# Rotary attention inputs with features in the order (dimension, head): half the rotary products, and six pack loads a unit for twelve

## The chip, the cores and the metric

The kernel runs on one core of a Trainium2 chip. The metric is the device time of one execution in microseconds (us). Names of engines: PE is the matrix engine (TensorE), DVE the VectorE, ACT the ScalarE, POOL the GpSimd, SP the SyncE, which here only issues DMAs. A "q" behind an engine's name (SPq, ACTq) is its DMA-issuing side. TensorE's clock has two levels, 1.2 and 2.4 GHz, and the profile gives the granted share of the higher one.

## The reference, cut to what matters

```python
# x: (8, 512, 256)   ctx: (8, 1601, 256)   16 heads of 16 dimensions
h = x + cross_attention(layernorm(x), ctx)        # weights Wq, Wk, Wv, Wo with biases
z = rmsnorm(layernorm(h), g1)
q, k, v = z @ wq, z @ wk, z @ wv                   # 16 heads of 16
q = q * cos + rotate_half(q) * sin                 # rotate_half([a, b]) = [-b, a], halves of 8
k = k * cos + rotate_half(k) * sin
a = causal_softmax(q @ k.T * 16 ** -0.5) @ v @ wo
... # residuals, a second rmsnorm, top-2 of 8 experts (256 -> 704 -> 256), residuals
```

## The kernel before

The work is done in stages with a barrier between them: prepare_weights, project_inputs, attention (cross), invert_denominators, project_self, attention (self, causal), invert_denominators, finish_self, route, experts. Matrices of fp32 precision are multiplied in bf16 where scores are made: every query and key feature is cut into three bf16 parts (high, middle, low), and the scores take six of the nine pairs of parts in one product over 6 x 16 = 96 rows of the contraction, with three more rows that subtract the row's maximum (99 in all).

project_inputs writes the parts to DRAM as k_parts and q_parts, shape (batch, 3 parts, 256 features, tokens). A feature's number is head * 16 + dimension.

attention works through 32 units, each one batch and four heads. For a unit, `load_kq` (L568 on) fills k_pack and q_pack, of 128 partitions x 4 heads x tokens. Each of the six pairs of parts takes 16 partitions (the dimension of the head), and each is filled by one DMA for the key and one for the query: 12 DMAs of 16 partitions, with a run of 3202 B (key, cross attention) or 1024 B (query, and key in self attention) for each head. SP issues, in order for each unit: the value loads for a later unit (L581, L585; runs of 64 B), the 12 pack loads for the unit three ahead (L570, L573), the store of the unit before (L590). Four pack buffers exist.

On PE the "pieces" (L637) are scores in the order (query, key) of which DVE takes the maxima (L718). They are spread by `step_of` over the steps of the unit before. POOL splits the maxima in three bf16 parts, PE turns them (L646), ACT copies them (L799) and sends them by a DMA of its own queue to rows 96 to 98 of q_pack (L804, the max-row transfer, 12 KB). The first scores of the next unit (L656) wait for that transfer; ACT then takes exponentials (L793), and PE the products with the values (L671). In self attention POOL also starts one load of expert weights a unit (L1855), on a third queue.

project_self handles a batch in each turn of a software pipeline (`turns`): each engine has a fixed list of parts, each for a batch some turns back. DVE's list is: subtract_high of k (b-3), residual (b-1), divide (b), rope of q (b-2), layer_norm (b-1), rms_inverse (b-1), subtract_high of q (b-2), rope of k (b-2). PE's list is: turn_rows (b-1), out_product (b), q_products (b-1), v_product (b-1), k_products (b-1). The rotation of halves is put into the weights: prepare_weights makes wq_rot and wk_rot, and rope_products multiplies with wq and wq_rot into ps_a and ps_b, which queries and keys share. DVE multiplies ps_a by the cosines and ps_b by the sines, POOL adds (L1137), ACT and DVE make the parts, SP stores them.

Of the kernel before, what the change touches and what calls it, by code (L numbers as in the profile page):

```python
# [17 lines left out]
GH = 4  # L18
# [19 lines left out]
K_PARTS = (0, 1, 2, 0, 1, 0)  # L38
Q_PARTS = (0, 0, 0, 1, 1, 2)
PAIRS = len(K_PARTS)  # L40
# [29 lines left out]
def prepare_weights(nc, w, keep):  # L70

    with ExitStack() as stack:
        p = Prog(nc, stack, "prep_")
        raw = {n: p.sb(f"raw_{n}", [P, KC, DIM]) for n in ("Wq", "Wk", "Wv", "Wo")}
# [6 lines left out]
        rot_ready = p.sem("rot_ready")  # L81

        with nc.Block() as block:
# [6 lines left out]
            @block.scalar  # L90
            def _(act):

                for n in ("bq", "bk", "g1"):
                    act.dma_start(keep[n][:, :], w[n].rearrange("(c p) -> p c", p=P),
                                  allow_slow_non_contiguous=True).then_inc(small_in, 16)
                for n in ("bv", "bo", "g2"):
                    act.dma_start(keep[n][:, :], w[n].partition_broadcast(P)).then_inc(small_in, 16)
                for n in ("wq", "wk", "wv", "wo"):
                    act.dma_start(keep[n][:, :, :], w[n].rearrange("(c p) o -> p c o", p=P)).then_inc(small_in, 16)
                act.dma_start(keep["w_router"][:, :, :], w["w_router"].rearrange("(c p) e -> p c e", p=P))\  # L100
                   .then_inc(small_in, 16)
                act.wait_ge(small_in, 16 * 11)

                nc.scalar.mul(keep["bq"][:, :], keep["bq"][:, :], SCALE)

                for src, dst in (("wq", "wq_rot"), ("wk", "wk_rot")):
                    s = keep[src][:, :, :].rearrange("p c (h t d) -> p (c h) t d", t=2, d=HD // 2)
                    d = keep[dst][:, :, :].rearrange("p c (h t d) -> p (c h) t d", t=2, d=HD // 2)
                    nc.scalar.mul(d[:, :, 0, :], s[:, :, 1, :], -1.0)
                    last = nc.scalar.copy(d[:, :, 1, :], s[:, :, 0, :])  # L110
                last.then_inc(rot_ready, 1)
                act.wait_ge(rot_ready, 1)
# [12 lines left out]
            @block.vector  # L125
            def _(dve):
                nc.vector.memset(keep["ln_eps"][:, :], LN_EPS)
                nc.vector.memset(keep["rms_eps"][:, :], RMS_EPS)
                for k, n in enumerate(("WqT", "WkT", "WvT", "WoT")):
                    dve.wait_ge(turned_ready, k + 1)  # L130
                    nc.vector.tensor_copy(keep[n][:, :, :], turned[k][:, :, :])
# [311 lines left out]
def attention(nc, q_parts, k_parts, v_rows, out_rows, kv, causal, keep, units, beside=None):  # L443
# [28 lines left out]
    with ExitStack() as stack:  # L472
# [30 lines left out]
        KQ = 16 * 2 * PAIRS  # L503
# [10 lines left out]
        class Unit:  # L514


            def __init__(self, i, r):
# [4 lines left out]
                self.rows = slice(g * GR, (g + 1) * GR)  # L522
# [42 lines left out]
        with nc.Block() as block:  # L565
            @block.sync
            def _(sp):
                def load_kq(v):  # L568
                    for r in range(PAIRS):
                        sp.dma_start(kp[v.buf][r * HD:(r + 1) * HD, :, :],  # L570
                                     k_parts[v.batch, K_PARTS[r], v.rows, :].rearrange("(j d) n -> d j n", d=HD))\
                          .then_inc(kq_in[v.buf], 16)
                        sp.dma_start(qp[v.buf][r * HD:(r + 1) * HD, :, :],  # L573
                                     q_parts[v.batch, Q_PARTS[r], v.rows, :].rearrange("(j d) n -> d j n", d=HD))\
# [305 lines left out]
def project_self(nc, x_in, out_rows, inverse, x1_rows, h0_rows, q_parts, k_parts, v_rows, keep, batches):  # L880


    with ExitStack() as stack:
# [19 lines left out]
        ps_a = p.ps("ps_a", [P, KC, SEQ])  # L903
        ps_b = p.ps("ps_b", [P, KC, SEQ])
# [30 lines left out]
        with nc.Block() as block:  # L935
# [43 lines left out]
            def _(pe):  # L979
# [17 lines left out]
                def rope_products(w, b):  # L997
                    pe.wait_ge(rope_read, b * 2 + w + 1)
                    for ps, weights in ((ps_a, ("wq", "wk")[w]), (ps_b, ("wq_rot", "wk_rot")[w])):
                        for o in range(KC):  # L1000
                            for i in range(KC):
                                last = nc.tensor.matmul(ps[:, o, :], keep[weights][:, i, o * P:(o + 1) * P],
                                                        xT[:, i, :], start=(i == 0), stop=(i == KC - 1))
# [21 lines left out]
            def _(dve):  # L1025
                for s in (on_ready, x1_ready, rope_read, *rest_ready):
                    dve.sem_inc(s, 1)

# [28 lines left out]
                def rope(w, b):  # L1057
                    dve.wait_ge(rope_done, b * 2 + w + 1)
                    dve.wait_ge(full_ready[w], b + 1)
                    for i in range(KC):  # L1060
                        nc.vector.tensor_tensor(t1[w][:, i, :], ps_a[:, i, :], keep["cos_" + "qk"[w]][:, :], ALU.mult)
                        last = nc.vector.tensor_tensor(t2[w][:, i, :], ps_b[:, i, :], keep["sin_" + "qk"[w]][:, :],
                                                       ALU.mult)
# [59 lines left out]
            def _(pool):  # L1123
# [10 lines left out]
                def add_and_split(w, b):  # L1134
                    pool.wait_ge(rope_read, b * 2 + w + 2)
# [682 lines left out]
def shape_constants():  # L1818
# [6 lines left out]
    cos = np.tile(np.cos(angle).T, (P // (HD // 2), 1)).astype(np.float32)  # L1825
    sin = np.tile(np.sin(angle).T, (P // (HD // 2), 1)).astype(np.float32)
# [35 lines left out]
KEEP_SHAPES = {"WqT": 0, "WkT": 0, "WvT": 0, "WoT": 0, "wq": 0, "wk": 0, "wv": 0, "wo": 0, "wq_rot": 0, "wk_rot": 0}  # L1862
# [80 lines left out]
```

## Time and profile before

| | |
|---|---|
| median of 3 runs | 3095.22 us (3091.45 to 3095.96) |
| the profiled execution, its own time | 3085.21 us |
| span of its profile | 3083.4 us |
| busy: PE, DVE, ACT, POOL | 87%, 59%, 47%, 19% |
| mean granted clock of TensorE | 0.928 |

The profile is of one execution. Its span is from the first to the last instruction. Where the page names what ended an idle time, that is the last of the things waited for. The stages lie, by the first loads of each, at 0 to 20 us (weights), to 290 (project_inputs), to 1581 (cross attention), to 1829 (the first inversion and project_self), to 2222 (self attention), to 2440 (finish_self and route) and to the end (experts).

### The profile page before, as it was taken

What the parts mean: (1) busy time and instruction counts of PE and PEld (TensorE: products, weight loads), DVE (VectorE), ACT (ScalarE), POOL (GpSimd) and SP (SyncE); (2) the same over time, 40 slices, a digit from 0 to 9 for tenths busy, and PEclk for the clock granted to TensorE, in tenths of its full rate; (3) what the DMA queues carried; (4) which work ended last, traced back from release to release, by engine and by line L of the source; (5) the groups of instructions that cost most, each with busy time, mean ns of one, the idle gap of its engine ahead of it and who ended that gap; (6) DMA issues with size and microseconds to landing.
All of it is one profiled execution on the core that took longest, in us unless ns stands there. A gap on an engine that the chain in (4) does not pass through costs nothing. (4 is left out here: it accounts for less than half of the span.)

```text
span 3083.4 us, 58524 instructions
## 1 busy us (share of the span) xinstructions
PE 2679.9 (87%) x14782; PEld 1368.5 (44%) x14783; DVE 1808.3 (59%) x3880; ACT 1441.9 (47%) x2927; POOL 589.0 (19%) x815
## 2 busy tenths in 40 slices
PE   7995999999999999999958968888634499999996
PEld 4663233333333333333315534444333467777775
DVE  4664988888878787878816645666423522222221
ACT  2332377777767676767742325665511022222221
POOL 2445000000000000000004441111022433333332
PEclk9998799999999999999979988999866699999998
DMA  6776654545554545454114656777444311121123
GB/s 205 224 224 159 69 61 62 61 62 61 62 62 61 62 62 62 61 62 61 19 55 160 202 125 124 132 133 138 95 153 150 98 31 32 31 33 31 31 33 73
DMA packets 496392, 279.26 MB, mean 91 GB/s; under 512 B 308992, under 2 KB 462480, under 8 KB 495984
## 3 DMA queue, kind: packets, MB, share of 16 engines
q1 hardware_dynamic: 465664, 235.90, 39.9%
q0 software_dynamic: 16192, 30.16, 5.1%
q10 hardware_dynamic: 14320, 10.63, 1.1%
q8 instruction: 98, 1.61, 0.2%
q14 instruction: 118, 0.97, 0.2%
HBM read 176.41 MB, written 103.57 MB: 91 GB/s over the span
## 5 line engine op out<-in xcount | busy, mean ns | idle before, releaser
L718 DVE TENSOR_REDUCE att_cross_neg_max<-att_cross_ps_s 128x1 f32<-128x401 f32 x2048 | 1031.0, 568 | 220.8 <-PE att_cross_ps_s L637 218.5
L793 ACT ACTIVATE att_cross_probs<-att_cross_ps_st 128x512 f32<-128x512 f32 (+1 forms) x1664 | 882.7, 601 | 340.4 <-PE att_cross_ps_st L656 322.5
L637 PE MATMUL att_cross_ps_s<-att_cross_k_pack,att_cross_q_pack 96*128 96x401 bf16 x2048 | 665.6, 348 | 30.0 <-DMA att_cross_q_pack<-q_parts 29.6
L656 PE MATMUL att_cross_ps_st<-att_cross_q_pack,att_cross_k_pack 99*128 99x512 bf16 (+1 forms) x1664 | 641.4, 389 | 34.9 <-issue 28.6
L671 PE MATMUL att_cross_ps_o<-att_cross_probs,att_cross_v_tiles 128*32 128x512 f32 (+1 forms) x3328 | 450.0, 613 | 0.1
L637 PEld LDWEIGHTS att_cross_ps_s<-att_cross_k_pack,att_cross_q_pack 96*128 96x128 bf16 x2048 | 203.1, 99 | 401.1 <-DVE att_cross_neg_max L718 238.1
L718 DVE TENSOR_REDUCE att_self_neg_max<-att_self_ps_s 128x1 f32<-128x128 f32 (+3 forms) x512 | 225.2, 486 | 159.9 <-PE att_self_ps_s L640 156.0
L656 PEld LDWEIGHTS att_cross_ps_st<-att_cross_q_pack,att_cross_k_pack 99*128 99x128 bf16 (+1 forms) x1664 | 165.4, 100 | 338.6 <-ACT att_cross_probs L793 192.8
L793 ACT ACTIVATE att_self_probs<-att_self_ps_st 128x256 f32<-128x256 f32 (+3 forms) x512 | 206.9, 440 | 146.7 <-PE att_self_ps_st L659 137.0
L1790 DVE COPY moe_hiddenT<-moe_ps_h 128x256 f32<-128x256 f32 x142 | 60.3, 424 | 297.0 <-PE moe_ps_h L1693 297.0
L764 POOL CAST att_cross_neg_max_parts<-att_cross_neg_max_merged 128x16 bf16<-128x16 f32 x32 | 6.3, 196 | 1188.9 <-DVE att_cross_neg_max_merged L711 1188.9
L1747 ACT ACTIVATE moe_silu<-moe_ps_g 128x352 f32<-128x352 f32 x142 | 65.7, 463 | 300.8 <-PE moe_ps_u L1685 300.8
L1703 PE MATMUL moe_ps_y<-top_wd_sb,moe_hiddenT 128*128 (+1 forms) x852 | 196.0, 379 | 1.1 <-DVE moe_hiddenT L1791 1.1
L656 PE MATMUL att_self_ps_st<-att_self_q_pack,att_self_k_pack 99*128 99x256 bf16 (+3 forms) x512 | 160.9, 316 | 41.3 <-DMA att_self_q_pack<-att_self_neg_max_rows 37.5
L1685 PE MATMUL moe_ps_g<-top_wg_sb,moe_rowsT 128*128 x568 | 192.8, 462 | 0.0
L1685 PE MATMUL moe_ps_u<-top_wu_sb,moe_rowsT 128*128 x568 | 191.9, 460 | 0.0
L637 PE MATMUL att_self_ps_s<-att_self_k_pack,att_self_q_pack 96*128 96x128 bf16 (+3 forms) x512 | 159.9, 316 | 31.0 <-DMA att_self_q_pack<-q_parts 29.9
L1703 PEld LDWEIGHTS moe_ps_y<-top_wd_sb,moe_hiddenT 128*128 128x128 f32 (+1 forms) x852 | 161.6, 190 | 35.1 <-issue 1.4
L1645 POOL DMA_INDIRECT sums<-moe_y,moe_target x71 | 113.4, 1597 | 281.3 <-ACT moe_y L1753 136.5
L1784 DVE TENSOR_TENSOR moe_hidden<-moe_ps_u,moe_silu 128x352 f32<-128x352 f32 x142 | 73.5, 517 | 132.8 <-ACT moe_silu L1747 131.2
L1685 PEld LDWEIGHTS moe_ps_u<-top_wu_sb,moe_rowsT 128*128 128x128 f32 x568 | 108.4, 191 | 60.7 <-issue 1.0
L671 PEld LDWEIGHTS att_cross_ps_o<-att_cross_probs,att_cross_v_tiles 128*32 128x32 f32 (+1 forms) x3328 | 66.4, 108 | 154.1 <-ACT att_cross_probs L793 129.3
(221 smaller groups left out, 3049.6 us busy)
## 6 DMA issues: line engine op xcount, KB each, us to landing
att_cross_k_pack<-k_parts SPq DMA_DIRECT2D x192, 200.1 KB, 6.8
k_parts<-in_part SPq DMA_DIRECT2D x72, 256.0 KB, 3.1
in_rows<-in_ctx_dram SPq DMA_DIRECT2D x24, 512.0 KB, 4.3
v_rows<-in_v_biased SPq DMA_DIRECT2D x24, 512.0 KB, 2.9
att_cross_q_pack<-q_parts SPq DMA_DIRECT2D x192, 64.0 KB, 7.7
att_cross_v_tiles<-v_rows SPq DMA_DIRECT2D x128, 96.0 KB
att_self_k_pack<-k_parts SPq DMA_DIRECT2D x192, 64.0 KB, 3.6
att_self_q_pack<-q_parts SPq DMA_DIRECT2D x192, 64.0 KB, 3.6
```

What stands on the lines that cost most here:

```text
L637: mm = nc.tensor.matmul(ps_s[bank][:, 0:w], qp[v.buf][0:SROWS, j, q * P:(q + 1) * P], kp[v.buf][0:SROWS, j, s:s + w], start=True, stop=not ...
L656: mm = nc.tensor.matmul(ps_st[bank_of_step[s]][0:rows, q0:SEQ], kp[u.buf][0:MROWS, j, t * P:t * P + rows], qp[u.buf][0:MROWS, j, q0:SEQ], ...
L671: nc.tensor.matmul(ps_o[j * VW:(j + 1) * VW, q0:SEQ], va[u.vbuf][0:rows, t, j, :], pr[0:rows, (u.odd * STEPS + t * GH + j) % RING, q0:SEQ] ...
L718: nc.vector.tensor_reduce(nmax[v.odd][:, j * QT + q, i:i + 1], ps_s[bank][:, 0:w], AX.X, ALU.max, negate=True).then_inc(s_read, 1)
L764: link(nc.gpsimd.tensor_copy(nm_parts[:, 0, :], full))
L793: nc.scalar.activation(pr[0:rows, (u.odd * STEPS + s) % RING, q0:SEQ], ps_st[bank_of_step[s]][0:rows, q0:SEQ], ACT.Exp).then_inc(exp_done, 1)
L1645: pool.indirect_dma_start(out=sums, in_=y[t.par][:, :], in_offset=None, compute_op=ALU.add, out_offset=bass.IndirectOffsetOnAxis(ap=target ...
L1685: last = nc.tensor.matmul(ps[half][:, 0:HHALF], xT[t.par][:, i, :], wt[:, bass.ds(at, HHALF)], start=(i == 0), stop=(i == KC - 1))
L1703: last = nc.tensor.matmul(ps_y[:, :], hT[half][0:CW[c], c, :], wd[0:CW[c], bass.ds(at, DIM)], start=(half == 0 and c == 0), stop=(half == ...
L1747: nc.scalar.activation(sil[half][:, :], ps_g[half][:, 0:HHALF], ACT.Silu).then_inc(sil_ready, 1)
L1784: nc.vector.tensor_tensor(h[half][:, :], ps_u[half][:, 0:HHALF], sil[half][:, :], ALU.mult)\
L1790: nc.vector.tensor_copy(hT[half][:, 0:CH - 1, :], ps_h[half][:, 0:CH - 1, :])
```

## The change

Query and key features take the number dimension * 16 + head. The weights' columns and the biases are reordered in prepare_weights; the values stay as they were. Three things follow in the code. First, the four heads of a unit lie beside each other in DRAM for each dimension, so a partition of a pack takes one run of 4 x tokens, and the pairs that share a query part are filled by one DMA: RUNS has 3, 2 and 1 pairs, so 48, 32 and 16 partitions, in the order (dimension, pair). Second, dimensions 0 to 7 are features 0 to 127, which is block 0 of the products, and dimensions 8 to 15 are block 1: the rotated half of a block is the other block, so the product with rotated weights is not made. Third, the two PSUM tiles become one for queries and one for keys, and a counter is moved by one for that.

```diff
-K_PARTS = (0, 1, 2, 0, 1, 0)
-Q_PARTS = (0, 0, 0, 1, 1, 2)
+RUNS = ((0, 3, 0), (3, 2, 1), (5, 1, 2))      # first pair, pairs, query part
...
# prepare_weights
-                for n in ("bq", "bk", "g1"):
-                    act.dma_start(keep[n][:, :], w[n].rearrange("(c p) -> p c", p=P), ...)
+                for n in ("bq", "bk"):
+                    for c in range(KC):
+                        act.dma_start(keep[n][:, c:c + 1], w[n].rearrange("(h c d) -> c d h", ...)[c].unsqueeze(2), ...)
+                act.dma_start(keep["g1"][:, :], ...)
...
-                for src, dst in (("wq", "wq_rot"), ("wk", "wk_rot")):
-                    nc.scalar.mul(d[:, :, 0, :], s[:, :, 1, :], -1.0)
-                    last = nc.scalar.copy(d[:, :, 1, :], s[:, :, 0, :])
+                for n in ("wq", "wk"):
+                    last = nc.scalar.copy(keep[n][:, :, :].rearrange("p c (d h) -> p c d h", d=HD),
+                                          raw[n][:, :, :].rearrange("p c (h d) -> p c d h", d=HD))
...
+                    if n in ("WqT", "WkT"):
+                        nc.vector.tensor_copy(keep[n][:, :, :].rearrange("p c (d h) -> p c d h", d=HD),
+                                              turned[k][:, :, :].rearrange("p c (h d) -> p c d h", d=HD))
...
# attention, load_kq
-                    for r in range(PAIRS):
-                        sp.dma_start(kp[v.buf][r * HD:(r + 1) * HD, :, :],
-                                     k_parts[v.batch, K_PARTS[r], v.rows, :].rearrange("(j d) n -> d j n", d=HD))
-                        sp.dma_start(qp[v.buf][r * HD:(r + 1) * HD, :, :],
-                                     q_parts[v.batch, Q_PARTS[r], v.rows, :].rearrange("(j d) n -> d j n", d=HD))
+                    for first, n, q_part in RUNS:
+                        at = slice(first * HD, (first + n) * HD)
+                        k = k_parts[v.batch, 0:n, :, :].rearrange("a (d h) n -> d a h n", d=HD)[:, :, v.heads, :]
+                        sp.dma_start(kp[v.buf][at, :, :], k.rearrange("d a h n -> d a (h n)"))
+                        q = q_parts[v.batch, q_part, :, :].rearrange("(d h) n -> d h n", d=HD)[:, v.heads, :]
+                        sp.dma_start(qp[v.buf][at, :, :],
+                                     q.rearrange("d h n -> d (h n)").unsqueeze(1).broadcast_to([HD, n, GH * SEQ]))
...
# project_self
-                    for ps, weights in ((ps_a, ("wq", "wk")[w]), (ps_b, ("wq_rot", "wk_rot")[w])):
-                        for o in range(KC):
-                            for i in range(KC):
-                                last = nc.tensor.matmul(ps[:, o, :], keep[weights][:, i, o * P:(o + 1) * P], ...)
+                    for o in range(KC):
+                        for i in range(KC):
+                            last = nc.tensor.matmul(ps_qk[w][:, o, :], keep[("wq", "wk")[w]][:, i, o * P:(o + 1) * P], ...)
...
                     for i in range(KC):
-                        nc.vector.tensor_tensor(t1[w][:, i, :], ps_a[:, i, :], keep["cos_" + "qk"[w]][:, :], ALU.mult)
-                        last = nc.vector.tensor_tensor(t2[w][:, i, :], ps_b[:, i, :], keep["sin_" + "qk"[w]][:, :], ALU.mult)
+                        nc.vector.tensor_tensor(t1[w][:, i, :], ps_qk[w][:, i, :], keep["cos_" + "qk"[w]][:, :], ALU.mult)
+                    nc.vector.scalar_tensor_tensor(out=t2[w][:, 0, :], in0=ps_qk[w][:, 1, :], scalar=-1.0,
+                                                   in1=keep["sin_" + "qk"[w]][:, :], op0=ALU.mult, op1=ALU.mult)
+                    last = nc.vector.tensor_tensor(t2[w][:, 1, :], ps_qk[w][:, 0, :], keep["sin_" + "qk"[w]][:, :], ALU.mult)
```

## Rows read from the trace of the kernel before

**Rows 1.** Busy time by stage: stretch, its length, each engine's us (xcount), clock, DMA share, GB/s.
```profile
20.10:289.90 269.80, 240.87 (x1008) 162.98 (x1008) 159.16 (x288) 94.75 (x174) 107.31 (x81) 0.97 0.68 209
289.90:1580.60 1290.70, 1237.66 (x7072) 404.37 (x7072) 1035.41 (x2080) 896.99 (x1729) 49.80 (x137) 0.95 0.48 59
1580.60:1828.80 248.20, 179.47 (x576) 106.11 (x576) 137.71 (x289) 69.47 (x105) 95.42 (x65) 0.88 0.48 155
1828.80:2222.50 393.70, 331.75 (x3104) 171.21 (x3104) 225.23 (x512) 224.10 (x577) 52.46 (x173) 0.93 0.68 127
```

**Rows 2.** What PE waited for, cross attention, 350 to 1540 us.
```profile
PE att_cross_ps_st L656 <- issue: 28.6, 12, 2.7
```

**Rows 3.** What PE waited for, self attention, 1864 to 2222 us.
```profile
PE att_self_ps_st L656 <- DMA att_self_q_pack<-att_self_neg_max_rows: 37.5, 28, 2.5
PE att_self_ps_s L637 <- DMA att_self_q_pack<-q_parts: 4.5, 7, 1.6
```

**Rows 4.** Timeline, start of cross attention (start, us, engine, line, what).
```profile
289.96 0.36 SPq L570 DMA_DIRECT2D att_cross_k_pack<-k_parts  x1
...
295.04 0.43 SPq L573 DMA_DIRECT2D att_cross_q_pack<-q_parts  x1
...
306.41 3.63 PE L637 MATMUL att_cross_ps_s<-att_cross_k_pack,att_cross_q_pack 96*128 96x401 bf16 x9 [29.55 <-DMA att_cross_q_pack<-q_parts]
```

**Rows 5.** DMA queues, 290 to 306.4 us: packets, MB, share of 16 engines.
```profile
q1 hardware_dynamic: 1081, 1.87, 101.5%
```

**Rows 6.** Timeline, start of self attention.
```profile
1828.87 0.36 SPq L570 DMA_DIRECT2D att_self_k_pack<-k_parts  x1
...
1837.30 0.29 PE L637 MATMUL att_self_ps_s<-att_self_k_pack,att_self_q_pack 96*128 96x128 bf16 x1 [25.43 <-DMA att_self_q_pack<-q_parts]
```

**Rows 7.** Timeline, a max-row transfer beside pack loads, and the last one with none.
```profile
1952.08 0.36 SPq L570 DMA_DIRECT2D att_self_k_pack<-k_parts  x1
...
1953.67 0.73 ACTq L804 DMA_DIRECT2D att_self_q_pack<-att_self_neg_max_rows  x1
...
1957.51 0.38 SPq L573 DMA_DIRECT2D att_self_q_pack<-q_parts  x1
...
1958.75 0.39 PE L656 MATMUL att_self_ps_st<-att_self_q_pack,att_self_k_pack 99*128 99x512 bf16 x1 [1.47 <-DMA att_self_q_pack<-att_self_neg_max_rows]
...
2206.28 0.73 ACTq L804 DMA_DIRECT2D att_self_q_pack<-att_self_neg_max_rows  x1
...
2209.47 0.39 PE L656 MATMUL att_self_ps_st<-att_self_q_pack,att_self_k_pack 99*128 99x512 bf16 x1 [0.40 <-DMA att_self_q_pack<-att_self_neg_max_rows]
```

**Rows 8.** DMA queues, 1950 to 1962 us; q0 is POOL's, q10 ACT's.
```profile
q0 software_dynamic: 80, 0.36, 9.8%
q10 hardware_dynamic: 51, 0.01, 1.1%
```

**Rows 9.** Timeline, project_self, one turn of the pipeline.
```profile
1698.26 1.09 PE L993 MATMUL slf_ps_t<-top_keep_constants,slf_x_rms 128*128 128x128 f32 x8 [1.47 <-ACT slf_x_rms L1094]
1699.19 3.62 PE L984 MATMUL slf_ps_o<-top_keep_WoT,slf_o_normed 128*128 128x256 f32 x16
...
1706.49 1.23 DVE L1037 TENSOR_TENSOR slf_x<-slf_ps_o,slf_x_biased 128x1024 f32<-128x1024 f32 x1 [0.50 <-DMA h_rows<-slf_h]
...
1721.83 1.09 PE L993 MATMUL slf_ps_t<-top_keep_constants,slf_x_rms 128*128 128x128 f32 x8 [1.47 <-ACT slf_x_rms L1094]
```

**Rows 10.** Timeline, project_self, where DVE's rope waits for PE: the first and the last batch.
```profile
1641.12 0.69 DVE L1061 TENSOR_TENSOR slf_rope_cos<-slf_ps_a,top_keep_constants 128x512 f32<-128x512 f32 x1 [0.91 <-PE slf_ps_b L1002]
...
1801.59 0.69 DVE L1061 TENSOR_TENSOR slf_rope_cos<-slf_ps_a,top_keep_constants 128x512 f32<-128x512 f32 x1 [1.90 <-PE slf_ps_b L1002]
...
1811.91 0.69 DVE L1061 TENSOR_TENSOR slf_rope_cos<-slf_ps_a,top_keep_constants 128x512 f32<-128x512 f32 x1 [3.07 <-PE slf_ps_b L1002]
```

**Rows 11.** Groups of instructions by form (busy us, mean ns of one | idle before).
```profile
L1002 PE MATMUL slf_ps_b<-slf_xT,top_keep_wq_rot 128*128 128x512 f32 x64 | 28.8, 592 | 0.0
...
L1416 DVE SCALAR_TENSOR_TENSOR route_probs<-route_first_choice,route_probs 128x256 f32<-128x256 f32 x1 | 0.4, 424 | 0.1
```

More of the change, by code:

```diff
@@ L33 @@
 RMS_EPS = 1e-6
-K_PARTS = (0, 1, 2, 0, 1, 0)
-Q_PARTS = (0, 0, 0, 1, 1, 2)
-PAIRS = len(K_PARTS)
+RUNS = ((0, 3, 0), (3, 2, 1), (5, 1, 2))
+PAIRS = sum(n for _, n, _ in RUNS)
 SROWS = PAIRS * HD
@@ L73, in prepare_weights @@
         p = Prog(nc, stack, "prep_")
-        raw = {n: p.sb(f"raw_{n}", [P, KC, DIM]) for n in ("Wq", "Wk", "Wv", "Wo")}
+        raw = {n: p.sb(f"raw_{n}", [P, KC, DIM]) for n in ("Wq", "Wk", "Wv", "Wo", "wq", "wk")}
         turned = [p.ps(f"turned{i}", [P, KC, DIM]) for i in range(4)]
@@ L130, in _ @@
                     dve.wait_ge(turned_ready, k + 1)
-                    nc.vector.tensor_copy(keep[n][:, :, :], turned[k][:, :, :])
+                    if n in ("WqT", "WkT"):
+                        nc.vector.tensor_copy(keep[n][:, :, :].rearrange("p c (d h) -> p c d h", d=HD),
+                                              turned[k][:, :, :].rearrange("p c (h d) -> p c d h", d=HD))
+                    else:
+                        nc.vector.tensor_copy(keep[n][:, :, :], turned[k][:, :, :])
                 dve.wait_ge(consts_in, 16)
@@ L521, in __init__ @@
                 g = r % GROUPS
-                self.rows = slice(g * GR, (g + 1) * GR)
+                self.heads = slice(g * GH, (g + 1) * GH)
                 self.columns = slice(g * GR, (g + 1) * GR)
@@ L902, in project_self @@
         ps_t = p.ps("ps_t", [P, KC, SEQ])
-        ps_a = p.ps("ps_a", [P, KC, SEQ])
-        ps_b = p.ps("ps_b", [P, KC, SEQ])
+        ps_qk = [p.ps(f"ps_qk{w}", [P, KC, SEQ]) for w in range(2)]
         att_in = p.sem("att_in")
@@ L998, in rope_products @@
                     pe.wait_ge(rope_read, b * 2 + w + 1)
-                    for ps, weights in ((ps_a, ("wq", "wk")[w]), (ps_b, ("wq_rot", "wk_rot")[w])):
-                        for o in range(KC):
-                            for i in range(KC):
-                                last = nc.tensor.matmul(ps[:, o, :], keep[weights][:, i, o * P:(o + 1) * P],
-                                                        xT[:, i, :], start=(i == 0), stop=(i == KC - 1))
+                    for o in range(KC):
+                        for i in range(KC):
+                            last = nc.tensor.matmul(ps_qk[w][:, o, :], keep[("wq", "wk")[w]][:, i, o * P:(o + 1) * P],
+                                                    xT[:, i, :], start=(i == 0), stop=(i == KC - 1))
                     last.then_inc(rope_done, 1)
@@ L1025, in _ @@
             def _(dve):
-                for s in (on_ready, x1_ready, rope_read, *rest_ready):
+                for s in (on_ready, x1_ready, *rest_ready):
                     dve.sem_inc(s, 1)
+                dve.sem_inc(rope_read, 2)
                 def divide(b):
```

39 lines of the change are left out of this document (21 added, 18 removed).

## The prediction

> **What bounds the kernel now.** I read the stages by windows first, then the list of what PE waited for in each attention, then the timelines at the places where something waits for a pack load or for the rotary products, and last the DMA queues there. By windows [rows 1] cross attention holds 1291 us with PE busy for 1238, and the waits of PE in it are 28.6 us in 12, none on a DMA [rows 2]. So the pack loads of its steady state are hidden, and only its start is open. Self attention holds 394 us with PE busy for 332. There PE waited 37.5 us, in 28 waits, for the max-row transfer, and 4.5 us, in 7, for pack loads [rows 3]. project_self (with the first inversion) holds 248 us with PE busy for 179: PE is not full there, and what goes round its loop has to be looked up. The experts' stage isn't touched.
>
> **Part 1, rotary products.** Two groups of 64 matmuls go, at 28.8 us each ([rows 11] has the queries; the keys' weights have the same shape), 57.6 us of PE. What of it is on the path? One turn of the pipeline goes from 1698.26 to 1721.83, 23.57 us. turn_rows waits for ACT's scaled rows; out_product follows at 1699.19 and is done at 1702.81; DVE's residual starts only at 1706.49, and its last wait was for the store of h0 [rows 9]. From there the turn runs over DVE and ACT (moments, normalisation, scaled rows) back to turn_rows. So PE is on this loop with turn_rows and out_product alone, which stay, and has 3.7 us of room. The rotary products lie beside it: 0 us in the seven full turns. At the ends they show: DVE's rope waits for ps_b 0.91 us in the first batch, and 1.90 and 3.07 us in the last [rows 10]. The first is won. In the last, the key's rope starts 3.07 us earlier at least, and up to 1.90 more if the query's gain came through POOL and ACT whole; POOL still has a split of the batch before to do, so I take 3.5. Sum: -4.4 us, between -4.0 and -5.9.
>
> The cover has a price: PE now works some 15 us of a turn and stands still for 8, so its clock will fall to the lower of its two levels between turns. At that level turn_rows and out_product take twice 1.09 and 3.62 us at most, 9.4 against 4.7, and the room of 3.7 us (out_product's end to the residual) would be passed by 1.0 us a turn, 7 us in all; since the clock rises again while the burst runs, I take 0 and keep 7 as the upper bound. DVE's four rope instructions stay four. One becomes scalar_tensor_tensor, which took 424 ns at 256 elements [rows 11] while the present one takes 690 ns at 512 [rows 10]; so it lies between 690 and 848 ns. Two a turn, both on DVE's list in front of the residual or the layer norm: 0 to 0.3 us a turn, 0 to 2.5 us in all, and I take 0, since the shorter one has the same cost a column with a fixed part beside it.
>
> **Part 2, weights.** Two more bias loads are issued by ACT (0.4 us each, as SP's in [rows 4]), and four copies read with a stride. The loads of the stage overlap, so +0.7 us, between 0 and +2.
>
> **Part 3, pack loads at the two starts.** At the start of cross attention nothing runs on PE until unit 0's 12 loads are in: from 289.96 (first issue) over 295.04 (last) to 306.41, 16.45 us for 6 x 200.1 + 6 x 64 KB = 1.62 MB [rows 4]. The last issue is 11 us old by then, so this is the rate of the transfers and not the issue: the queue moved 1.87 MB in 16.4 us, 114 GB/s, with all 16 engines counted as busy [rows 5]. project_inputs moves 209 GB/s at a share of 0.68 [rows 1], in transfers over all 128 partitions. The new loads are the same bytes in 48, 32 and 16 partitions and in runs four times as long. Bounds: the old rate (0 us won) and the 307 GB/s that 209 at 0.68 would make of a full share (5.3 us, some 9 us won with 2 us of latency). I take the 209 of the stage's own rows: 7.8 + 2.0 us for 16.45, so -6.5 us. The pieces that follow run at DVE's pace and move as a whole.
>
> At the start of self attention, 768 KB in 12 loads take 8.43 us from first issue to first piece [rows 6]. The issue of 12 at 0.47 us is 5.6 us of it; six take 2.8. At 209 GB/s the bytes take 3.8, with 2 us latency 5.8: -2.7 us, between 0 and -3.5.
>
> The Trainium skill ("SBUF — State Buffer", section on the DMA port swizzle) says that a transfer into 16 neighbouring partitions reaches 4 of 16 ports, about 109 GB/s, and one into 32 or 48 reaches 8, about 218. The 114 GB/s of [rows 5] agrees. By that rule five sixths of the bytes would go at 218 and one sixth at 109, 8.8 us for 1.62 MB, which would make the cross start -5.7 in place of -6.5.
>
> **Part 4, the steady state of self attention.** This is the largest term and the least sure. A max-row transfer issued at 1953.67, amid pack loads that SP issued from 1952.08 to 1957.51, let PE start at 1958.75, 5.1 us later; the last one, issued at 2206.28 with no pack loads, let PE start at 2209.47, 3.2 us later [rows 7]. POOL's load of expert weights stood beside both; of q10's 51 packets in that stretch none is large (0.01 MB) [rows 8]. So pack loads cost the transfer about 1.9 us, and of that PE waits 37.5 / 28 = 1.34 us a unit [rows 3]. Six loads are issued in 2.8 us instead of 5.4, and their bytes are gone some 2 to 3 us earlier, about 1957 in this unit; but they still begin before the transfer does. Bounds: all waits stay (0) and all go (-37.5). In the best case the transfer is as quick as the last one, earlier than PE needs; in the worst it waits until the pack loads have drained, now about 1.5 us earlier. I take 60%, since half of the transfer's time still lies beside the loads: -22 us. The 7 waits for pack loads themselves go, as the loads land earlier: -4.5 us, between 0 and that.
>
> In cross attention nothing is behind a pack load, and I take 0 for the 28.6 us of "issue" [rows 2]: those are waits for no transfer of data.
>
> **Sum.** -4.4 + 0.7 - 6.5 - 2.7 - 22 - 4.5 = -39.4 us. Against the profiled execution (3085.2 us, 1.8 beyond its span) that is 3046; its median stands 10.0 us above it, so the forecast for the median is 3095.2 - 39.4 = 3056.
>
> **Rivals.**
> A. The max-row waits stay. For it: the transfer is issued only 1.6 us after the first pack load and still meets the burst. Against it: the burst ends earlier. The rest is -4.4 + 0.7 - 6.5 - 2.7 = -12.9 and perhaps some of the 4.5: 3080.
> B. All of them go. For it: the two ends of [rows 7] differ by 1.9 us and PE waits for 1.34. Then -55: 3040.
> C. The pack loads are no faster; what limits them isn't the number of partitions or the length of a run but something that both forms share (the read side, or the engines' own rate). For it: an engine share of 101.5% doesn't say where the time is spent. Then only the rotary ends and a little issue time are left: -4 to -6: 3090.
> D. Slower: the transfer queues behind longer runs. A run of the pack loads grows from 1 KB to 4 KB in self attention. Were the 17 packets that each of three engines has for the transfer to wait for a run each, and the burst not shorter, the transfer would land later. The price: each us later is 28 us. With 1.5 us it is +42 - 12.9 = +29: 3124. It decides from 0.7 us on (12.9 + 6.2 over 28). Against it: the burst has a fixed number of bytes, after which nothing is in the way.
>
> The Trainium skill ("DMA: Bandwidth & Descriptors", section on queues, rings and completion order) says that an engine takes turns between its queues by the packet. That is the rule by which D would come true; [rows 8] shows the queues side by side, but not the order in them.
>
> **How the numbers follow.** Forecast (part of the waits goes, 3045 to 3072) 0.50, A 0.18, B 0.14, C 0.10, D 0.08. A measurement of this kernel can tell about 0.2%, 6.2 us, from no change. Forecast, A and B are faster, 0.82; C lies across the bound and I count most of it as no change: same 0.10; slower 0.08, D and nothing else. The range has to take in the forecast's own bounds, B and A: 3038 to 3088. Outside are C's upper part and D.
>
> **What the profile of the changed kernel would show.** The first piece of cross attention 9 to 10 us after the first pack load, not 16.5; that of self attention 6 us, not 8.4. The list of waits in self attention: for the max-row transfer about 15 us, not 37.5 (near 0 is B, 37 or more is A, above 50 is D). project_self's turn still at 23 to 23.6 us, with PE some 15 us busy in it, a lower granted clock, and its end 3 to 5 us earlier than its start. Cross attention's steady units unchanged. What would make this wrong: a turn of project_self longer than 23.6 us (the clock, or scalar_tensor_tensor), or pack loads still at 114 GB/s.

## The result, and the profile after

The changed kernel took 3131.84 us (median of 4, 3126.45 to 3135.08) against 3095.59 us of the kernel before: slower by a factor of 1.0118, 95% interval 1.0101 to 1.0136. The forecast was 3056 with a range up to 3088. The profiled execution took 3132.67 us, its span is 3130.8 us, 47.4 us more than before, and its mean granted clock 0.912, not 0.928.

The busy time by stage of the kernel after (stretch, length, busy us of PE, PEld, DVE, ACT and POOL, clock, DMA share, GB/s), to be read against [rows 1]:

```profile
290.10:1580.40 1290.30, 1239.44 (x7072) 404.25 (x7072) 1035.49 (x2080) 896.91 (x1729) 49.82 (x137) 0.95 0.39 59
1580.40:1825.80 245.40, 139.48 (x448) 94.40 (x448) 137.71 (x289) 69.45 (x105) 95.45 (x65) 0.79 0.48 157
1825.80:2267.60 441.80, 358.43 (x3104) 183.92 (x3104) 224.61 (x512) 227.44 (x577) 52.20 (x173) 0.87 0.55 113
```

Cross attention is as long as it was. project_self lost 40 us of PE's busy time (57.6 us of products are gone, and the rest takes longer at a clock of 0.79 in place of 0.88) and became 2.8 us shorter. Self attention is 48 us longer: 441.8 us for 393.7. It has the same 3104 products on PE, which now take 358 us for 332, at a clock of 0.87 for 0.93. The list of what PE waited for there, from 1860 to 2267 us (us in total, times, longest), beside [rows 3]:

```profile
PE att_self_ps_st L663 <- DMA att_self_q_pack<-att_self_neg_max_rows: 66.7, 29, 3.1
```

The waits for pack loads are gone, and those for the max-row transfer have grown from 37.5 to 66.7 us. One unit shows how (timeline of the kernel after, start, us, engine, line, what), to be read against [rows 7]:

```profile
1954.77 0.60 SPq L577 DMA_DIRECT2D att_self_k_pack<-k_parts  x1
1955.47 0.57 SPq L580 DMA_DIRECT2D att_self_q_pack<-q_parts  x1
1955.89 0.73 ACTq L811 DMA_DIRECT2D att_self_q_pack<-att_self_neg_max_rows  x1
1956.13 0.57 SPq L577 DMA_DIRECT2D att_self_k_pack<-k_parts  x1
...
1958.43 0.38 SPq L580 DMA_DIRECT2D att_self_q_pack<-q_parts  x1
...
1961.51 0.39 PE L663 MATMUL att_self_ps_st<-att_self_q_pack,att_self_k_pack 99*128 99x512 bf16 x1 [2.02 <-DMA att_self_q_pack<-att_self_neg_max_rows]
```

The transfer is issued at 1955.89, and PE starts 5.62 us later; in the unit of [rows 7] it was 5.08. Over the units of the stage the medians of this time are 6.02 us and 4.81. By the transfer's issue SP has handed over (its issuing instruction has ended) one load of 192 KB here, in other units two, and has begun a further one; in the kernel before it was two to four of 64 KB, and in most units one begun.

What the transfer waits for shows in the DMA queues between its issue and the start of its first packet, 3.16 us in this unit and 1.95 us in that of [rows 7] (q0 is POOL's queue, q1 SP's; q10, ACT's, isn't listed, as it moved nothing). Kernel after, 1955.89 to 1959.04 us, then kernel before, 1953.67 to 1955.61 us:

```profile
q1 hardware_dynamic: 128, 0.39, 45.9%
q0 software_dynamic: 80, 0.36, 43.5%
```

```profile
q0 software_dynamic: 79, 0.36, 60.7%
q1 hardware_dynamic: 206, 0.17, 26.3%
```

POOL's queue moves the same in both. SP's moves 0.39 MB here, which is the two loads of 192 KB that were handed over or begun, and 0.17 MB in the kernel before. What the wait does to PE stands in the windows of 1 us around its end (kernel after; the clock is the third number from the end):

```profile
1960.00:1961.00 1.00, 0.00 (x0) 0.00 (x0) 0.00 (x0) 0.00 (x0) 0.00 (x0) 1.00 0.99 184
1961.00:1962.00 1.00, 0.49 (x3) 0.27 (x4) 0.00 (x0) 0.00 (x0) 0.00 (x0) 1.00 0.89 221
1962.00:1963.00 1.00, 1.00 (x8) 0.59 (x7) 0.73 (x2) 0.93 (x2) 0.00 (x0) 0.71 0.26 90
1963.00:1964.00 1.00, 1.00 (x7) 0.66 (x6) 0.58 (x2) 0.82 (x2) 0.00 (x0) 0.50 0.00 0
1964.00:1965.00 1.00, 1.00 (x11) 0.23 (x9) 0.47 (x2) 0.60 (x1) 0.00 (x0) 0.50 0.00 0
```

PE had stood still for 2.02 us; from 1962.3 on it has half its clock for some 3 us and makes 7 or 11 products in a microsecond. In the kernel before, behind the wait of 1.47 us of [rows 7], two such windows show 1.00 and 16 or 17 products:

```profile
1960.00:1961.00 1.00, 1.00 (x16) 0.55 (x14) 0.93 (x4) 1.00 (x3) 0.00 (x0) 1.00 0.48 147
1961.00:1962.00 1.00, 1.00 (x17) 0.65 (x10) 0.60 (x2) 0.83 (x3) 0.00 (x0) 1.00 0.01 4
```

So a unit went from 11.1 to 13.6 us (median between two transfers), by more than the transfer itself lost.

The two starts (timelines of the kernel after), for [rows 4] and [rows 6]:

```profile
290.19 0.73 SPq L577 DMA_DIRECT2D att_cross_k_pack<-k_parts  x1
...
303.15 8.93 PE L644 MATMUL att_cross_ps_s<-att_cross_k_pack,att_cross_q_pack 96*128 96x401 bf16 x20 [26.07 <-DMA att_cross_q_pack<-q_parts]
...
1825.88 0.68 SPq L577 DMA_DIRECT2D att_self_k_pack<-k_parts  x1
1826.62 0.61 SPq L580 DMA_DIRECT2D att_self_q_pack<-q_parts  x1
...
1833.26 0.29 PE L644 MATMUL att_self_ps_s<-att_self_k_pack,att_self_q_pack 96*128 96x128 bf16 x1 [25.75 <-DMA att_self_q_pack<-q_parts]
```

From the first pack load to the first piece it is 12.96 us in place of 16.45, and 7.38 in place of 8.43. A wide load takes 0.6 to 0.7 us of SP, a narrow one took 0.36 to 0.43 with its gap at 0.47.

project_self, one turn and its last batch on PE (timeline of the kernel after), for [rows 9] and [rows 10]:

```profile
1697.82 1.97 PE L999 MATMUL slf_ps_t<-top_keep_constants,slf_x_rms 128*128 128x128 f32 x8 [6.25 <-ACT slf_x_rms L1103]
1699.58 5.32 PE L990 MATMUL slf_ps_o<-top_keep_WoT,slf_o_normed 128*128 128x256 f32 x16
...
1721.92 1.97 PE L999 MATMUL slf_ps_t<-top_keep_constants,slf_x_rms 128*128 128x128 f32 x8 [6.71 <-ACT slf_x_rms L1103]
...
1795.32 5.30 PE L1007 MATMUL slf_ps_qk<-slf_xT,top_keep_wq 128*128 128x512 f32 x8 [1.36 <-ACT slf_xT L1109]
```

PE now stands still for 6 us a turn and does turn_rows in 1.97 us, not 1.09, and out_product in 5.32, not 3.62: the granted clock is 0.50 in the first and 0.68 over the second. All of that fits in front of DVE's residual, and the turn is 24.1 us here; over six turns it is 140.53 us (1651.46 to 1791.99) for 139.97 before.

The difference of the spans, taken from the starts of the same instructions in both traces: to the end of cross attention -0.1 us; from there to the first piece of self attention -3.9 (-2.9 to its first pack load, -1.0 behind it); self attention, from its first piece to its last product on the values, 428.75 for 379.59, +49.2; the rest +2.3. Sum +47.4.

### The profile page after: what moved, and what is told of

Read it like the earlier page. It is cut to its first block and busy times, and to the rows that moved or that the text cites. A ratio compares the mean times of both kernels' runs of the same rounds, so it can differ in the third digit from the quotient of the medians.

```text
span 3130.8 us, 57492 instructions
## 1 busy us (share of the span) xinstructions
PE 2672.1 (85%) x14654; PEld 1370.8 (44%) x14655; DVE 1806.3 (58%) x3880; ACT 1446.1 (46%) x2925; POOL 588.4 (19%) x815
## 5 line engine op out<-in xcount | busy, mean ns | idle before, releaser
L663 PE MATMUL att_self_ps_st<-att_self_q_pack,att_self_k_pack 99*128 99x256 bf16 (+3 forms) x512 | 174.9, 344 | 69.0 <-DMA att_self_q_pack<-att_self_neg_max_rows 66.7
L644 PE MATMUL att_self_ps_s<-att_self_k_pack,att_self_q_pack 96*128 96x128 bf16 (+3 forms) x512 | 171.0, 338 | 26.0 <-DMA att_self_q_pack<-q_parts 25.7
```

What stands on the lines that cost most here:

```text
L644: mm = nc.tensor.matmul(ps_s[bank][:, 0:w], qp[v.buf][0:SROWS, j, q * P:(q + 1) * P], kp[v.buf][0:SROWS, j, s:s + w], start=True, stop=not ...
L663: mm = nc.tensor.matmul(ps_st[bank_of_step[s]][0:rows, q0:SEQ], kp[u.buf][0:MROWS, j, t * P:t * P + rows], qp[u.buf][0:MROWS, j, q0:SEQ], ...
```

## The experiments

All that are timed stand beside runs of the kernel before on the same chip, 3 rounds each. "Transfer" is the median, over the units of self attention, of the time from the issue of the max-row transfer to PE's first scores of the unit (where the transfer is quick, PE sets this time itself, at 3.54 us; only units at the ends of the stage show less, as the last of [rows 7] with 3.19). "Unit" is the median time between two transfers. "Stage" is from the first piece of self attention to the last product on the values.

| run | us | ratio to before, interval | transfer | unit | PE waits for transfer | clock | stage |
|---|---|---|---|---|---|---|---|
| before_again | 3089.33 | | 4.76 | 11.2 | 37.4 | 0.95 | 378.0 |
| after | 3131.84 | 1.0118 (1.0101 to 1.0136) | 6.02 | 13.6 | 66.7 | 0.88 | 428.8 |
| after_again | 3126.78 | | 5.76 | 13.3 | 60.9 | 0.89 | 418.8 |
| twelve_long | 3096.71 | 0.998 (0.9962 to 0.9997) | 5.31 | 11.5 | 48.5 | 0.92 | 395.4 |
| twelve_short | 3095.38 | 0.9979 (0.9966 to 0.9993) | 5.26 | 11.6 | 43.9 | 0.92 | 390.4 |
| fill8 | 3095.93 | 0.9982 (0.9969 to 0.9995) | 5.84 | 11.9 | 10.5 | 0.99 | 387.1 |
| spaced | 3114.42 | 1.0080 (1.0054 to 1.0106) | 5.50 | 12.9 | 54.9 | 0.90 | 406.0 |
| light_first | 3067.86 | 0.9931 (0.9905 to 0.9958) | 4.53 | 10.6 | 31.3 | 0.95 | 362.4 |
| swap_after | 3032.38 | 0.9777 (0.9761 to 0.9794) | 3.68 | 9.7 | 4.4 | 0.98 | 325.3 |
| swap_before | 3044.11 | 0.9853 (0.9829 to 0.9877) | 3.79 | 9.9 | 8.5 | 0.97 | 332.6 |
| behind | 3058.42 | 0.9887 (0.9866 to 0.9907) | 3.54 | 10.7 | 1.4 | 0.99 | 349.8 |
| behind_before | 3140.02 | 1.0156 (1.0132 to 1.0179) | 3.58 | 13.5 | 2.7 | 0.88 | 428.7 |
| values_last | 3106.41 | 1.0044 (1.0027 to 1.0061) | 5.39 | 12.9 | 51.4 | 0.91 | 398.4 |

**Is it the length of a run?** That was rival D of the prediction. twelve_long and twelve_short have 12 narrow loads again in self attention, the first with runs of 4 KB, the second with 1 KB.

```diff
+                    if causal:
+                        for r in range(PAIRS):
+                            at = slice(r * HD, (r + 1) * HD)
+                            k = k_parts[v.batch, (0, 1, 2, 0, 1, 0)[r], :, :].rearrange("(d h) n -> d h n", d=HD)[:, v.heads, :]
+                            sp.dma_start(kp[v.buf][at, :, :], k).then_inc(kq_in[v.buf], 16)
...
+                        return
-    k2_parts = dram("k2_parts", [batches, 3, DIM, SEQ], BF16)
+    k2_parts = dram("k2_parts", [batches, 3, DIM, SEQ + 32], BF16)[:, :, :, 0:SEQ]
```

The first part is in both (q_parts are loaded alike, with parts 0, 0, 0, 1, 1, 2), the last two lines, and the same for q2_parts, in twelve_short alone.

> The changed kernel with 12 pack loads of 16 partitions a unit in self attention only; the runs stay 4 KB. Before, the max-row transfer took 5.0 us from issue to PE's start and a unit 11.5 us; after, 6.0 and 13.6. Theory R (a transfer's packets take turns with packets of 4 KB in place of 1 KB): the transfer stays at about 6.0 us, a unit at 13.5, the time at 3125 to 3135. Rival G (fewer and wider loads fill the queue more densely at that moment): the transfer goes back to 5.0, a unit to 11.5, the time to about 3085.

> The changed kernel with 12 pack loads of 16 partitions in self attention, and the rows of its query and key parts in DRAM 1088 bytes apart for 1024, so that a run is 1 KB again; this is the pattern of loads of the kernel before under the changed project_self. R and G: transfer 5.0 us, unit 11.5, time about 3085 to 3090 (the gain at the two starts and the rotary ends stays). If something else of the change slows self attention: transfer 6.0, time 3125 or more.

The transfer took 5.31 and 5.26 us (5.0 expected by G), and the times are 3096.7 and 3095.4 (3085 to 3090 expected) against 3099.9 of before on that chip. Runs of 4 KB cost the transfer nothing that can be seen; theory R falls, and with it the mechanism of rival D. What matters is that the bytes come in six wide loads. The queue of twelve_long, 1860 to 2150 us (the last number is us from issue to landing):

```profile
q1 hardware_dynamic: 63047, 27.71, 51.8%
...
att_self_k_pack<-k_parts SPq DMA_DIRECT2D x143, 64.0 KB, 3.5
```

The same view and stretch of the kernel after:

```profile
att_self_k_pack<-k_parts SPq DMA_DIRECT2D x22, 192.0 KB, 3.7
att_self_q_pack<-q_parts SPq DMA_DIRECT2D x22, 192.0 KB, 5.1
...
att_self_k_pack<-k_parts SPq DMA_DIRECT2D x22, 128.0 KB, 5.3
```

A narrow load lands 3.5 us after its issue, and a wide one, from the second on, 5 us: SP hands over 192 KB in 0.7 us, and the loads stand in line. Left open is that both runs' stage is 11 to 17 us above that of the kernel before; their chip ran the kernel before 11 us slower than the next one did, and no profile of it from that chip exists.

**What does the clock cost?** fill8 has 8 products on PE ahead of its wait for the transfer, whose result nothing reads.

```diff
+                    if causal and before:
+                        pe.wait_ge(exp_done, u.n * STEPS - bank_age(0) + 4)
+                        for _ in range(FILL):
+                            nc.tensor.matmul(ps_st[bank_of_step[0]][:, :], kp[u.buf][0:SROWS, 0, 0:P],
+                                             qp[u.buf][0:SROWS, 0, :], start=True, stop=True)
                     pe.wait_ge(m_rows_in, (u.n + 1) * 16 + 1)
```

> The changed kernel with 8 products of 512 columns (1.8 us at the higher clock) added on PE ahead of its wait for the max-row transfer in self attention, whose result nothing reads. Theory C (of the 2.1 us that a unit is longer than before, 1.0 is the transfer and 1.0 the lower clock that PE has after waits of 2 us and more): granted clock in self attention near 1.0, unit 12.5, time about 3100. Rival: the clock is not what lengthens the unit; the time stays at 3130 or grows.

The transfer stays at 5.84 us, but the unit goes from 13.6 to 11.9 us. The stage of fill8 (its window from the first piece to the last product):

```profile
1837.04:2224.15 387.11, 370.73 (x3337) 188.27 (x3337) 221.49 (x512) 220.96 (x575) 45.42 (x168) 0.99 0.61 125
```

At a clock of 0.99 it is 42 us shorter than the kernel after, with some 250 more products. So theory C holds, and the clock's part was larger than the 1.0 us a unit that I gave it: 1.7. The same shows unit by unit. Behind 28 of the 30 waits of more than 0.4 us for the transfer the granted clock fell to the lower level in the kernel after, behind 7 of 28 in the kernel before, and behind 1 of 14 in fill8.

**Does the work in front of the transfer count, or the wide load itself?** spaced issues each of the six loads two steps of PE after the last one; light_first reverses their order, so that SP has handed over 128 KB by the transfer's issue and has begun 128 more; in the kernel after it is 192 KB, in some units 384, and in most of them a further load begun (the expectations count the load that is begun).

```diff
+                            sp.wait_ge(st_done, base + min(7 + 2 * i, STEPS))
...
-                    for first, n, q_part in RUNS:
+                    for first, n, q_part in (RUNS[::-1] if causal else RUNS):
```

> The changed kernel; in self attention each of the six wide pack loads of a unit is issued two steps of PE (about 1.3 us) after the one before, which is about the pace in bytes that 12 narrow loads have. Theory Q (wide loads hand the engines 192 KB an issue, more than they move in that time, so that work stands in front of the max-row transfer on its engines): the transfer goes back to 5.0 to 5.3 us, unit under 12, time 3080 to 3105. Rival W (a wide load itself, its 48 partitions or its repeated reading of a query part, slows the transfer): the transfer stays at 6.0, unit 13.5, time 3125 or more.

> The changed kernel with the six pack loads of self attention in the reverse order: 64, 64, 128, 128, 192, 192 KB. What has been issued by the time of the max-row transfer is 128 KB in place of 384 KB; the total is the same. Q: transfer between 5.0 and 5.6, time 3095 to 3115. If the transfer ends when the whole burst ends: 6.0, time 3130.

The first line is spaced's (i counts the loads), the last two are light_first's. spaced: 5.50 us and 3114, both in between. In the unit looked at, SP had begun its second load of 192 KB 0.24 us ahead of the transfer, for 0.42 in the kernel after, and the fourth load came 1.9 us behind it, for 1.0. The same wide loads at a slower pace do less harm. light_first: 4.53 us, and 0.69% faster than before; both are better than the 5.0 to 5.6 us and 3095 to 3115 that theory Q had given it. One unit of it (timeline):

```profile
1952.73 0.36 SPq L577 DMA_DIRECT2D att_self_k_pack<-k_parts  x1
...
1953.28 0.33 SPq L580 DMA_DIRECT2D att_self_q_pack<-q_parts  x1
1953.70 0.62 SPq L577 DMA_DIRECT2D att_self_k_pack<-k_parts  x1
1953.83 0.74 ACTq L811 DMA_DIRECT2D att_self_q_pack<-att_self_neg_max_rows  x1
...
1958.28 0.39 PE L663 MATMUL att_self_ps_st<-att_self_q_pack,att_self_k_pack 99*128 99x512 bf16 x1 [0.85 <-DMA att_self_q_pack<-att_self_neg_max_rows]
```

The same six wide loads with the same bytes start as far ahead of the transfer, 1.1 us, and PE starts 4.45 us behind its issue. That the transfer ends when the burst ends is thereby refuted. Rival W isn't, by this run alone: the two loads of 192 KB are issued last, 1.4 and 2.0 us behind the transfer. The table of packets below bears on it.

**And work behind it?** behind and behind_before hold the pack loads until 12 steps of the unit are done.

```diff
-                            sp.wait_ge(st_done, u.n * STEPS + RING)
+                            sp.wait_ge(st_done, u.n * STEPS + RING + (12 if causal else 0))
```

> The changed kernel; SP holds the six pack loads of self attention until PE has made 12 steps of the unit, which is about 1 us after the max-row transfer is issued, so that none is ahead of it and all of them run while it is in flight. If what counts is the work that stands in front of the transfer when it is issued (theory Q): transfer 3.7 to 4.3 us, waits of PE under 25 us in all, unit about 10.5, time 3035 to 3065. If the engines share their time between the queues as long as both have packets, whatever came first: transfer 5.3 us or more, time 3090 or more.

> The kernel before with the same hold on its 12 pack loads. Q: transfer 3.7 to 4.3 us, time 3045 to 3070. Sharing: transfer 4.8 us as before, time 3090.

In a unit of behind all of the burst is issued between the transfer's issue and PE's start (timeline):

```profile
1951.38 0.74 ACTq L811 DMA_DIRECT2D att_self_q_pack<-att_self_neg_max_rows  x1
1952.08 0.62 SPq L577 DMA_DIRECT2D att_self_k_pack<-k_parts  x1
...
1955.60 0.33 SPq L580 DMA_DIRECT2D att_self_q_pack<-q_parts  x1
```

and the transfer takes its least time, 3.54 us. Loads issued 0.7 us and more behind it cost it nothing. But this says nothing on how two queues share the engines. From the transfer's issue to 1953.10 us the queues show:

```profile
q0 software_dynamic: 61, 0.25, 38.1%
q10 hardware_dynamic: 51, 0.01, 3.2%
```

All 51 packets of the transfer are through, and no packet of a pack load has started. The packets, counted unit by unit in the traces, split the transfer's time in three (medians of 28 units, us; "in front" is what SP's queue moved between the transfer's issue and its first packet):

| run | in front, MB | issue to first packet | first to last packet | last packet to PE's start |
|---|---|---|---|---|
| behind | 0 | 1.38 | 0.26 | 1.89 (PE's own) |
| before | 0.18 | 2.11 | 1.05 | 1.68 |
| light_first | 0.19 | 2.28 | 0.62 | 1.56 |
| twelve_short | 0.19 | 2.19 | 1.25 | 1.74 |
| twelve_long | 0.21 | 2.24 | 1.07 | 1.67 |
| swap_after | 0.28 | 2.68 | 0.38 | 0.68 |
| spaced | 0.37 | 3.11 | 0.82 | 1.65 |
| values_last | 0.43 | 3.33 | 0.59 | 1.46 |
| after | 0.44 | 3.29 | 1.04 | 1.65 |

The 1.2 us between the kernels before and after lie in the first part alone, and that part grows with the bytes in front at 209 to 240 GB/s, narrow loads and wide ones alike. So a wide load does no more harm per byte than a narrow one, which speaks against rival W. Where pack loads move beside the transfer or just behind it, the other two parts together take 2.0 to 3.0 us, in swap_after 1.1; they are the same before and after, and no run separates what makes them long.

What PE waited for, in behind and then in behind_before:

```profile
PE att_self_ps_s L644 <- DMA att_self_q_pack<-q_parts: 23.5, 25, 1.3
PE att_self_ps_st L663 <- DMA att_self_q_pack<-att_self_neg_max_rows: 1.4, 2, 1.0
```

```profile
PE att_self_ps_s L637 <- DMA att_self_q_pack<-q_parts: 60.0, 28, 2.7
PE att_self_ps_st L656 <- DMA att_self_q_pack<-att_self_neg_max_rows: 2.7, 3, 1.5
```

I had expected 3045 to 3070 of behind_before, and it took 3140: the 12 loads now land too late for the pieces, which PE needs at the fifth step of the next unit, and the waits of 2.1 us each cost the clock too (0.88). Under this hold the change is worth 82 us (3058 for 3140), because six loads are issued in 3.9 us and twelve in 5.6.

**Out of the way on the other side.** swap_after and swap_before issue the pack loads at the start of the unit, ahead of the value loads.

```diff
+                    if causal and after >= 3:
+                        if before:
+                            sp.wait_ge(st_done, u.n * STEPS + RING)
+                        load_kq(u.next(3))
                     if after >= VBUFS - 1:
...
-                    if after >= 3:
+                    if not causal and after >= 3:
```

> The changed kernel; in self attention SP issues the six pack loads ahead of the value loads, as soon as the unit before has its scores, which is at the unit's start and 4 to 5 us earlier than now. Theory (it is the pack loads that the transfer meets): transfer 4.3 us or less, waits of PE under 1 us a unit, unit 11 us, time 3055 to 3075. Rival V (the value loads, in runs of 64 bytes, or POOL's load of weights slow it as much): transfer 5 us or more, time 3090 to 3125.

> The kernel before with pack loads issued ahead of the value loads in self attention, as in swap_after (3032 us). Its 12 loads take 5.6 us to issue from the unit's start and end just when the max-row transfer is issued, the six of the change take 4. If the change is worth something once its pack loads are out of the transfer's way, this one has a transfer of 4 to 4.5 us and a time of 3045 to 3070; if the change is worth nothing there, 3032 to 3040.

swap_after is the fastest kernel of this study, 2.2% below before, and both runs are a little faster than expected (3055 to 3075, and 3045 to 3070). Its stage and its waits:

```profile
PE att_self_ps_st L667 <- DMA att_self_q_pack<-att_self_neg_max_rows: 4.4, 12, 0.8
...
1832.26:2157.57 325.31, 315.19 (x3088) 166.69 (x3088) 221.53 (x512) 220.85 (x575) 45.10 (x167) 0.98 0.72 149
```

The value loads, with runs of 64 B, and the store of 256 KB stand right in front of the transfer here, and it takes 3.68 us, so rival V doesn't explain the wait. They aren't free: its first packet starts 2.68 us after the issue, for 1.38 in behind, but PE's own 3.54 us cover most of that. Of the two kernels the changed one is faster by 0.8% (0.9777 / 0.9853), some 24 us. The spans of the two profiles, of two chips, differ by 18.2 us: 4.7 up to the first piece of cross attention, 4.2 in that stage, 2.0 from there to the first piece of self attention, 7.3 in self attention, and nothing behind it.

**Do the value loads take part?** values_last issues the pack loads at their present time and the value loads behind them.

```diff
+                    if causal and after >= 3:
+                        if before:
+                            sp.wait_ge(st_done, u.n * STEPS + RING + 7)
+                        load_kq(u.next(3))
                     if after >= VBUFS - 1:
...
```

> The changed kernel; in self attention SP issues the six pack loads at the same moment as now (about 1.1 us ahead of the max-row transfer, held by PE's seventh step), and the four value loads behind them in place of in front. If the pack loads in front of the transfer are all that delays it: transfer 5.7 to 6.0 us, unit 13.3, time 3115 to 3135. If it is the pack loads on top of the value loads (2048 runs of 64 bytes, whose end they meet): transfer 4.5 us or less, time 3050 to 3085, and the wide loads land 3.8 to 4.2 us after their issue in place of 5.

Neither number came out: 5.39 us and 3106. With the unit shorter, PE's seventh step came earlier against the transfer, and in the unit looked at the loads started 2.3 us ahead of it, not 1.1, so the run changed two things. It shows that the wait persists with no value load in front, and its first packet starts as late as in the kernel after (3.33 us behind 0.43 MB, 3.29 behind 0.44). So the value loads add nothing to that part; whether they lengthen the rest stays open.

**The two repeats for their profiles:**

> The kernel before once more, for a profile on the same chip as these runs: self attention 380 to 395 us, max-row transfer 5.0 us.

> The changed kernel once more, for a profile beside these: max-row transfer 6.0 us, self attention about 430 us, time 3125 to 3135.

Both are near: before_again's stage is 378 us (380 to 395 expected) and its transfer 4.76 us (5.0), after_again's 419 (430) and 5.76 (6.0).

## Why the prediction was wrong

**The step that failed is part 4**, the steady state of self attention, -22 us forecast. I had read rightly that the pack loads cost the transfer time, and had concluded that the burst's earlier end would make it quicker: "six loads are issued in 2.8 us instead of 5.4, and their bytes are gone some 2 to 3 us earlier". What counts is the other end of the burst, the work that stands in front at the transfer's issue. Its first packet starts only when that work has moved: 1.38 us after the issue with nothing in front (behind), 2.11 behind 0.18 MB (before), 3.29 behind 0.44 MB (after). Six wide loads put more in front in the same time (192 KB in 0.7 us, where the narrow ones of [rows 7] are 64 KB in 0.47), so each transfer lost about 1.2 us, which is +29.2 us of waits. What SP has handed over by the issue is only a rough count of it, as some has moved by then: in the kernel after the time is 5.98 us in the 14 units with one load handed over and one begun, and 6.09 in the 10 with two and one; in the kernel before it is 5.05 us in the 12 units with two and one, and about 4.8 in the 6 with four.

**A second term was missing there: the clock.** I had priced it for project_self alone. With waits of 2.3 us on the average in place of 1.3, PE ran at the lower level behind 28 of them, not 7, and took 26 us more for the same products (358.4 for 331.8). 29.2 + 26.6 is 55.8; less the 4.5 us of pack waits it is 51, and the stage grew by 49.2.

**The 7 waits for pack loads**, -4.5: right, none is left.

**Rival D** had 0.08 and a time of 3124, near the 3132 measured, and its signature (waits above 50 us) came true. Its place was right, the transfer behind the loads, but the cause, the length of a run, was not, as twelve_long shows; nor did it have the clock. The runs speak against turns by the packet as what sets the added delay here: packets of 4 KB don't lengthen it (5.31 us for 5.26), and in the unit above SP's queue moved 0.39 MB, and ACT's nothing, before the transfer's first packet. The Trainium skill's rule of turns ("DMA: Bandwidth & Descriptors", queues, rings and completion order) may hold once both have packets at an engine, which no row here shows; it doesn't give the size of this wait.

**Part 1, rotary products**, -4.4, at least -4.0: the last subtraction of DVE went from 1817.92 to 1814.59, and 0.2 of these 3.3 us were there when the stage began (its first load of the attention's output at 1593.21 for 1593.42), so it is -3.1, short of my bound. The turns stayed as forecast, 23.4 for 23.3 us, at the lower clock, within PE's room. I had looked for the cover's price in the turns; it came at the end: the last batch's turn_rows took 1.97 us in place of 1.09 and its q_products 5.30 in place of 3.70. scalar_tensor_tensor takes 0.68 us, as the multiplication it replaced; 0 was right.

**Part 2, weights**: +0.2 at the first pack load, where I had 0.7.

**Part 3, cross attention's start**, -6.5: -3.5, inside the bounds. The queue moved 2.03 MB in 13.2 us (290 to 303.2 us), 154 GB/s at a share of 93.5%, faster than 114 but not 209. The Trainium skill's rule ("SBUF — State Buffer", the DMA port swizzle) had given -5.7, also too much (summed again from its figures the bytes take 8.7 us, an estimate, where I wrote 8.8). That the gain would last, as the pieces "move as a whole", did not show either. The 3.3 us by which PE began earlier had shrunk to 0.1 by the stage's end, and by steps: the max-row transfers of the two traces stand 2.7 us apart up to unit 5, 1.3 from unit 6, 0.9 from unit 10, and 0.2 from unit 26, each step at a turn of the loop. From first piece to last product the stage took 1271.5 to 1277.7 us in the ten traces with the changed loads (median 1275.4) and 1271.2 to 1275.7 in the four with the old ones (median 1272.0). The ranges overlap, but the medians are as far apart as the start had won. So no gain of this start reached the end of the stage, and why stays open.

**Self attention's start**, -2.7: -1.05. A wide load takes SP 0.7 us from one issue to the next; I had used the 0.47 of a narrow one, so that six take 4.1 us to issue and not 2.8.

## What to carry to other kernels

Where a small transfer is waited for, look at what other queues still have to move at the moment of its issue, and not at how long they stay busy: fewer and larger loads make a burst shorter but put more in front. A coarser load is safe to try once it has been moved away from the transfer, before or behind, as far as its own readers allow; here a swap in SP's order was worth 3.4% where the change had cost 1.2%. And price a wait by what it does to PE's clock as well: waits longer by 1.0 us (66.7 / 29 for 37.5 / 28) lengthened a unit by 2.5.

## What the runs showed of the hardware

- A max-row transfer of 12 KB on ACT's queue took PE from 3.54 us (pack loads issued 0.7 us behind it) to 6.02 us (one or two loads of 192 KB handed over on SP's queue ahead of it, and a further one begun), with the same loads. The difference before its first packet is 1.38 to 3.29 us, for 0 to 0.44 MB that SP's queue moved first (behind, after).
- From one issue to the next a load of 64 KB in 16 partitions costs SP 0.47 us (before); one of 128 or 192 KB with runs of 4 KB in 32 or 48 partitions 0.64 to 0.7 (after).
- PE stood still for 1.47 us in one unit (before) and kept a granted clock of 1.00; after 2.02 us in another (after) it had 0.50 for about 3 us. No single length divides the two: a wait of 1.51 us was followed by the lower level and one of 2.30 us wasn't (both in the kernel after). Eight products ahead of such a wait, whose result nothing reads (fill8), brought the stage from 0.88 to 0.99 and the kernel from 1.0118 to 0.9982 of before.
- Packets of 4 KB in place of 1 KB lowered the share of time of SP's queue from 57.1% to 51.8% at 12 loads and about the same bytes (twelve_short and twelve_long, 1860 to 2150 us), without any effect on the transfer.
